# Two column blocks of the first linear stage side by side, its input in two halves

## The reference, cut to what matters

```python
styles = w @ (affine_w * gain).T + affine_b
ws = weight[None] * styles[:, None, :]
dcoefs = rsqrt(sum(ws * ws, axis=2) + 1e-08)
y = einsum('blc,oc->blo', x * styles[:, None, :], weight) * dcoefs[:, None, :]
x = x + clip(y + bias, -256, 256)                     # L0
kx = modulated_linear(x, s, k...)                     # K: the same form, without the clip
A = softmax(einsum('bnhd,bnjd->bnhj', kx, kx) / sqrt(D))
out = modulated_linear(einsum('bnhj,bnjd->bnhd', A, kx), s, o...)   # O
x = x + out
```

## Time and profile before

| | |
|---|---|
| median of 3 runs | 717.39 us (715.54 to 717.6) |
| profiled execution, its own time | 716.73 us |
| its span, first to last instruction | 714.9 us |
| mean granted TensorE clock | 0.990 |
| PE busy | 693.1 us (97%), 8914 matmuls |
| DVE, ACT, POOL busy | 580.8, 544.8, 115.6 us |

### The profile page before, as it was taken

The page is one execution under the profiler, slowest core; times in us unless marked ns, Lnnn a source line. Parts: engine busy times, 40 slices in busy tenths (PEclk is TensorE's granted clock), DMA queues, the critical chain, the costliest instruction groups (busy, mean ns, idle before and its releaser), DMA issues.

```text
span 714.9 us, 21692 instructions
## 1 busy us (share of the span) xinstructions
PE 693.1 (97%) x8914; PEld 674.8 (94%) x8914; DVE 580.8 (81%) x1048; ACT 544.8 (76%) x1072; POOL 115.6 (16%) x107
## 2 busy tenths in 40 slices
PE   8999998999999999999999999999999999989796
PEld 8999998999999999999999999999999999989685
DVE  3678987889888888988888998888898788886762
ACT  5897877887777888777788887778886777875663
POOL 2021211111101111110111111011111011111100
PEclk9999999999999999999999999999999999999899
DMA  8357987488767677877777887776778777666663
GB/s 290 116 146 188 239 207 216 142 218 223 196 190 191 200 209 212 225 185 201 192 206 204 222 213 182 206 192 203 204 218 215 180 187 204 192 188 178 164 193 118
DMA packets 229667, 140.39 MB, mean 196 GB/s; under 512 B 141248, under 2 KB 223168, under 8 KB 229568
## 3 DMA queue, kind: packets, MB, share of 16 engines
q1 hardware_dynamic: 229568, 139.00, 71.4%
HBM read 71.85 MB, written 67.11 MB: 194 GB/s over the span
## 4 chain that ended last, share of the span: by engine, by line
PE 53%; DMA 14%; ACT 13%; DVE 10%; SPq 6%; issue 4%; ACTq 0%; DVEq 0%
PE lin_ps L415 43%; PE y_ps L479 5%; DMA k_turned<-kx 4%; PE s_ps L461 4%; DMA yr<-y_turned 4%; DMA y_turned<-y 4%; ACT p_bd L591 3%; ACT kx L503 2%; ACT x_hi L512 2%; SPq L239 2%; SPq L255 2%; ACT y_hi L512 2%; SPq L263 1%; ACT o L503 1%; DVE x_lo L687 1%
## 5 line engine op out<-in xcount | busy, mean ns | idle before, releaser
L415 PE MATMUL lin_ps<-x_hi,w_hi 128*128 128x256 f32 x1008 | 287.8, 286 | 4.9 <-ACT x_hi L512 3.0
L415 PE MATMUL lin_ps<-x_lo,w_hi 128*128 128x256 f32 x1008 | 282.0, 280 | 0.0
L415 PE MATMUL lin_ps<-x_hi,w_lo 128*128 128x256 f32 x1008 | 281.7, 279 | 0.0
L415 PEld LDWEIGHTS lin_ps<-x_hi,w_hi 128*128 128x128 f32 x1008 | 190.1, 189 | 14.8 <-issue 11.2
L385 POOL COPY k_bd<-k_rhs 32x1024 f32<-32x1024 f32 x96 | 111.3, 1159 | 556.4 <-DVE k_rhs L744 552.6
L415 PEld LDWEIGHTS lin_ps<-x_lo,w_hi 128*128 128x128 f32 x1008 | 190.2, 189 | 0.0
L415 PEld LDWEIGHTS lin_ps<-x_hi,w_lo 128*128 128x128 f32 x1008 | 190.1, 189 | 0.0
L512 ACT ACTIVATE x_hi<-x,style 128x256 fp32r<-128x256 f32 x252 | 113.1, 501 | 62.6 <-DVE x L765 56.0
L687 DVE SCALAR_TENSOR_TENSOR x_lo<-x,style,x_hi 128x256 fp32r<-128x256 f32 x252 | 146.7, 633 | 14.2 <-ACT x_hi L512 14.2
L415 PE MATMUL lin_ps<-y_hi,w_hi 128*128 128x256 f32 x528 | 150.6, 285 | 5.9 <-DVE y_lo L687 4.0
L415 PE MATMUL lin_ps<-y_lo,w_hi 128*128 128x256 f32 x528 | 149.3, 283 | 0.0
(11 more groups left out here) (61 smaller groups left out, 735.9 us busy)
## 6 DMA issues: line engine op xcount, KB each, us to landing
x<-xT SPq DMA_DIRECT2D x32, 512.0 KB, 5.8
k_turned<-kx SPq DMA_DIRECT2D x32, 512.0 KB, 2.9
k_st<-k_turned SPq DMA_DIRECT2D x128, 128.0 KB, 3.1
v_turned<-k_rhs SPq DMA_DIRECT2D x32, 512.0 KB, 6.1
k_v<-v_turned SPq DMA_DIRECT2D x128, 128.0 KB, 3.6
y_turned<-y SPq DMA_DIRECT2D x128, 128.0 KB, 3.3
yr<-y_turned SPq DMA_DIRECT2D x32, 512.0 KB, 4.7
outT<-o SPq DMA_DIRECT2D x31, 512.0 KB, 4.3
```

Of the source, the lines that this page charges most:

```text
L415: mm = pe.matmul(lin_ps[:, n % NLB, 0:T], w[:, k, m * P:(m + 1) * P], r[:, k, :], start=(q == 0), stop=(q == len(passes) - 1))
```

## The change

Three edits. First, at the start: SP loads x of chunk 0 in two halves, each followed by two weight quarters, with a semaphore for each half; PE takes the first two column blocks together, so that each of the 12 passes is issued for both blocks before the next pass; and there are 19 instead of 24 dummies behind the style product. Second, as a consequence, the counts on the semaphore of the even chunks of x are one lower, since chunk 0 no longer raises it. Third, far from the start, in the last third of `act_head`: the evacuation of the last K block of chunk 5 (`k_out` 3) comes before the spreads 2 and 3 of chunk 3, and `copy_keys` of chunk 4 after them.

```diff
-    WARM_STYLES, WARM_L0 = 9, 24
+    WARM_STYLES, WARM_L0 = 9, 19
...
-            [("warm", WARM_STYLES)] + one("styles", L0) + [("warm", WARM_L0)] + blocks(L0, 0, [0, 1]) + one("norms", L0)
+            [("warm", WARM_STYLES)] + one("styles", L0) + [("warm", WARM_L0)] + [("lin", L0, 0, 0, 2)] + one("norms", L0)
...
+            def load_first_x(h):
+                ks = slice(h * KB // 2, (h + 1) * KB // 2)
+                sp.dma_start(x_sb[:, 0, ks], xT_v[:, ks, 0:T]).then_inc(ld_x0[h], DMA)
...
-            load_x(0)
-            for h in range(parts[L0]):
-                load_weights(L0, h)
+            for h in range(2):
+                load_first_x(h)
+                load_weights(L0, 2 * h)
+                load_weights(L0, 2 * h + 1)
             load_x(1)
...
-                    mm = pe.matmul(lin_ps[:, n % NLB, 0:T], w[:, k, m * P:(m + 1) * P], r[:, k, :],
-                                   start=(q == 0), stop=(q == len(passes) - 1))
-                mm.then_inc(pe_lin, 1)
+                    for j in range(width):
+                        mm = pe.matmul(lin_ps[:, (n + j) % NLB, 0:T], w[:, k, (m + j) * P:(m + j + 1) * P], r[:, k, :],
+                                       start=(q == 0), stop=(q == len(passes) - 1))
+                        if q == len(passes) - 1:
+                            mm.then_inc(pe_lin, 1)
...
-                act.wait_ge(ld_x[c % 2], DMA * (c // 2 + 1))
+                if c == 0:
+                    act.wait_ge(ld_x0[h], DMA)
+                else:
+                    act.wait_ge(ld_x[c % 2], DMA * (c // 2 + c % 2))
...
-                (3, spread_some, 0), (5, k_out, 2), (3, spread_some, 1), (4, copy_keys), (3, spread_some, 2),
-                (3, spread_some, 3), (5, k_out, 3), (1, o_out, 0), (1, o_out, 1), (1, o_out, 2), (1, o_out, 3),
+                (3, spread_some, 0), (5, k_out, 2), (3, spread_some, 1), (5, k_out, 3), (3, spread_some, 2),
+                (3, spread_some, 3), (4, copy_keys), (1, o_out, 0), (1, o_out, 1), (1, o_out, 2), (1, o_out, 3),
```

More of the change, by code:

```diff
@@ L138, in build @@
         ld_x = [sem(f"ld_x{i}") for i in range(2)]
+        ld_x0 = [sem(f"ld_x0_{h}") for h in range(2)]
         v_out_landed, v_in_landed = sem("v_out_landed"), sem("v_in_landed")
@@ L198, in build @@
             if step[0] == "lin":
-                block_no[step[1:]] = len(block_no)
+                l, c, m, *width = step[1:]
+                for j in range(m, m + sum(width or [1])):
+                    block_no[(l, c, j)] = len(block_no)
         def done(l, c, m):
@@ L395, in _, with linear @@
             split = {L0: (a_xhi, v_xlo), K: (a_x1hi, v_x1lo), O: (a_yhi, v_ylo)}
-            def linear(l, c, m):
+            def linear(l, c, m, width=1):
                 n = block_no[(l, c, m)]
```

## The result

| kernel | runs | median us | lowest to highest | ratio to the kernel before | 95% interval |
|---|---|---|---|---|---|
| before | 7 | 717.39 | 714.74 to 717.88 | | |
| changed | 7 | 711.86 | 709.43 to 714.23 | 0.9930 | 0.9906 to 0.9953 |
| changed, again, beside the experiments | 12 | 711.73 | 708.64 to 716.27 | 0.9946 | 0.9917 to 0.9976 |

The sign was right, the size too small: 3.0 us were forecast, 5.5 us came in the first comparison of medians and 4.1 us in the second.

What follows compares the result with a forecast made beforehand. The prediction took PE's pace in the loop as the bound, so that gains in the head reach the end. From a base of 717.39 us, 1.3 + 1.67 = 3.0 us gave 714.4 us, range 712.6 to 716.8.

Steps and rivals of the forecast that it cites:

- What bounds the kernel, and that the gains add up: Whole kernel: the loop runs at PE's pace, so gains in the head move the end; 1.3 + 1.67 = 3.0 us.
- The loads: Start: six 256 KB pieces keep the stream's landing places; x's first half at 7.7 us, quarter 3 at 11.3.
- the first term: Gain from the start, up to K's norms: 1.3 us, bounds 0.8 and 1.6.
- The rival in which the second half of x lands at 10.9 us or later: Start: no stream for halves, ACT's squares 0.5 us later, first gain 0.3 us, 715.4 us in all; chance 0.13.
- ACT and DVE at the start: Start: ACT's squares end at 13.73 us, 0.47 won; DVE's last w_lo at 12.83, 0.66 won.
- PE at the start: Start: third quarter at 12.4 us, norms at about 14.0 against 15.6, 1.6 us early; fewer dummies worth 0.1 us.
- PE's 1.6 us don't all arrive: Start to K's norms: evacuation 0.94 us earlier, then ACT's squares hold norms to 24.85 us, leaving 1.3 us.
- all engines are the same 1.3 us early: From K's norms on: every engine keeps the 1.3 us, and nothing there waits for a transfer from the start.
- The three steps of ACT: Near 109.5 us: PE's 2.04 us wait goes, a 0.37 us wait for POOL comes ahead of the scores.
- the second term: Gain from ACT's new order near 109.5 us: 2.04 - 0.37 = 1.67 us, bounds 0 and 2.04.
- the clock falls at the start: Start: fewer dummies and shorter work bring PE's lower clock, costing up to 10.0 us, 724.1 us in all; chance 0.05.

Runs made afterwards that it cites:

- the two halves: Kernel before with the third edit alone, mean gain 2.7 ± 1.4 us; changed kernel without the third edit, mean gain 1.8 ± 1.6 us.
- the start alone: Changed kernel without the third edit (ACT's list in the old order), against the kernel before: median 715.70 us, ratio 0.9979, mean gain 1.8 ± 1.6 us.

## Why the prediction was too small, by its steps

**What bounds the kernel, and that the gains add up: right.** Both gains are there, in the head, and the means of the two halves add up to that of the whole. One reading of the earlier trace rows is off without a number hanging on it: DVE carries that chain to 12.90 us; 13.49 is the end of its last w_lo in the timeline.

**The loads: wrong, and the first term mis-sized by it.** The prediction gave the six pieces "the landing of its place" in a stream that it took as fixed, and so ended with "no more, since quarter 3's landing is fixed". That is the step that failed: with x in halves quarter 3 landed at 10.5 us, not 11.3, and x's first half at 6.7, not 7.7. ACT's squares ended at 12.99 (forecast 13.73), DVE's last w_lo at 12.19 (12.83). The rival in which the second half of x lands at 10.9 us or later is out: it landed at 9.1, and the halves and quarters came 0.6 to 1.1 us apart. Why the whole stream came sooner stays open; that it did is in all eight profiles with the halves around quarters 0 and 1.

**ACT and DVE at the start: right in kind.** First x_hi at 6.92 instead of 7.72 us, and then DVE's style, not x, is the last input, which the prediction didn't name.

**PE at the start: mis-sized for another reason.** The prediction called the dummies "no brake" and had PE wait for the third quarter at 12.4 us. The low parts were ready sooner (the last w_lo ends at 12.19), so PE had no pause from the dummies' end at 10.51, not 9.9, to `norms` at 13.52, where 14.0 was forecast. The dummies were a brake here, but 0.50 us of their lateness is scatter: they began at 6.14 us, not 5.64, and in fourteen profiles they begin anywhere from 5.6 to 6.3.

**"PE's 1.6 us don't all arrive": wrong.** ACT was to be the brake at K's `norms` with 24.85 us; its first evacuation starts 1.78 us earlier rather than 0.94, its squares end at 24.02, and PE arrives at 24.09 without a wait. The path was right: DVE does go into `norm_t` straight from y_lo of chunk 1. But y_lo starts 1.21 us earlier (13.82 instead of 15.03), not 0.47, so this error too goes back to the loads. First gain at that point 2.07 us instead of 1.3. Between 50 and 65 us some is lost, against "all engines are the same 1.3 us early": DVE waits 1.28 us instead of 0.54 for `k_st`, first before, then in the changed kernel,

```profile
56.01 1.09 DVE L744 COPY k_rhs<-k_st 128x1024 f32<-128x1024 f32 x1 [0.54 <-DMA k_st<-k_turned]
...
54.73 1.10 DVE L757 COPY k_rhs<-k_st 128x1024 f32<-128x1024 f32 x1 [1.28 <-DMA k_st<-k_turned]
```

and from there the changed kernel is 1.24 us ahead of the kernel before in this pair of profiles. That part varies: scores of chunk 1 start 62.9 to 64.2 us in six profiles of the new start and 65.4 to 68.0 in four of the old one (68.0 in the one whose clock fell at the start). The measured 1.8 ± 1.6 us for the start alone can't tell 1.3 from 2.05.

**The three steps of ACT: right, and the second term likely mis-sized.** Wait gone, POOL's in its place (0.51 to 0.56 us in seven profiles, forecast 0.37), 1.72 us of gain in the pair of profiles. But the "2.04 us" were read from an execution whose clock happened to hold. In four of six the wait is followed by the lower clock, which costs another 1.55 to 1.76 us (20.53 to 20.74 against 18.98). On the mean that is 4/6 x 1.6 = 1.1 us, an estimate from six profiles, and the second gain 1.67 + 1.1 = 2.8 us; measured 2.7 ± 1.4, which 1.67 would fit too. With 1.24 to 2.07 of the first it makes 4.0 to 4.9 us, and the runs give 4.1 ± 1.6 and 5.1 ± 1.5 (means). From the base of 717.39 these terms lead to 712.5 to 713.4 us, at the lower edge of the range; that the median of seven runs came out at 711.86 is within the scatter.

**The rivals.** That a pause brings the lower clock was priced only where the change might add one, "the clock falls at the start". The pause of 2.04 us that the change removes, of nearly the length of the 2.66 us in the earlier trace rows, was not asked the same question. At the start the clock stayed 1.00 in all seven profiles of the new start, and it was the old start that lost it once. The Trainium skill (TensorE: Matmul & The Clock Gate, "The HAM clock gate") says that the slow clock is the default and activity releases it; the runs agree in kind, and show that behind a pause of 2.0 us the lower clock came in four profiles and not in two.

**Still open.** Behind the head, the two profiled executions differ by another 4.3 us of span, in the loop's own stalls and in the tail, where the clock over 600 to 700 us is 0.95 to 0.99 in kernels with the same code there. That is scatter between executions as far as these runs tell; whether the changed kernel holds its clock in the tail more often isn't settled.

## What to carry to other kernels

A wait of PE costs more than its length if PE is slow behind it: look at the spacing of the weight loads after each pause, and in more than one profile, since one execution can be the lucky one. Cutting a load in two where its first half can be used moves not only that half: what stands behind it may land sooner too, so a landing time is no constant of its place. And three runs say little about the scatter: here 35 runs of one kernel spread over 10 us where the first three spread over 2.

## What the hardware did that I had not expected

- The same pause of 2.0 us was followed by a fall of TensorE's granted clock in four of six profiles, and in the one profile with 16 spare matmuls in it the clock stayed at 1.00. A pause of 0.98 us at the start was followed by a fall in one profile (0.84 over 9 to 20 us) and by none in the profile of the kernel before, nor was one of 1.01 us with 13 dummies.
- Moving the same 512 KB of x in two transfers let the 256 KB quarter at the end of the queue land 0.5 to 1.6 us sooner (10.2 to 10.7 us against 11.2 to 11.8, in eight and five profiles), where the bytes ahead of it were the same.
